# A plan of two pairs a step while the loop fills, and x3 turned at the end of a step

## The reference

```
x = layernorm(x + L1(x, edges))            # for a row: x1 + leaky(scale * p + shift)
x = layernorm(x + L2(x, edges, ...))       # equivariant layer; ssp(x) = softplus(x) - log 2
x = layernorm(x + L3(x, edges))            # q, k, v = x @ W; softmax of q.k over the edges of a source
```

## Time and profile before

| | |
|---|---|
| time, median of 3 runs | 2155.87 us (2149.54 to 2156.42) |
| the profiled execution | 2156.94 us, span 2155.2 us |
| busy share of the span | PE 84%, DVE 67%, ACT 53%, POOL 44% |
| mean granted TensorE clock | 0.896 |
| the last phase | from 1643 us of the span to its end |

### The profile page before, as it was taken

One profiled execution on the slowest core, in us unless ns is written; L12 is line 12 of the kernel. 1 busy time (PEld: TensorE's weight loads), 2 busy tenths in 40 slices (PEclk: granted clock), 3 DMA queues, 4 the chain that ended last, 5 costly groups with the idle time before them and its releaser, 6 DMA issues. The chain is left out here.

```text
span 2155.2 us, 24520 instructions
## 1 busy us (share of the span) xinstructions
PE 1803.9 (84%) x5525; PEld 933.2 (43%) x5525; DVE 1434.7 (67%) x2621; ACT 1149.2 (53%) x2356; POOL 949.1 (44%) x1070
## 2 busy tenths in 40 slices
PE   5999999599999999999999995961881588998840
PEld 2444444244444444444444443531771344544420
DVE  5365554177777777777777773517995578787876
ACT  1344434255555555555555552224883878877853
POOL 2212102166666666656666663544553232333236
PEclk8999999799999999999999997985555689999965
DMA  7752102534444454444444445554556887878774
GB/s 250 250 206 63 27 13 31 142 134 172 171 159 166 157 172 172 165 164 155 169 172 172 163 153 188 105 87 156 110 119 178 257 242 221 238 212 241 200 212 144
DMA packets 167421, 350.61 MB, mean 163 GB/s; under 512 B 30481, under 2 KB 30962, under 8 KB 166838
## 3 DMA queue, kind: packets, MB, share of 16 engines
q1 hardware_dynamic: 130838, 247.28, 32.4%
q0 software_dynamic: 33168, 98.01, 20.4%
q10 hardware_dynamic: 3344, 4.51, 0.7%
HBM read 177.32 MB, written 153.71 MB: 154 GB/s over the span
## 5 line engine op out<-in xcount | busy, mean ns | idle before, releaser
L687 PE MATMUL d_p_h<-w3a,d_xT 128*128 128x512 f32 x632 | 285.6, 595 | 23.2 <-DMA d_xT<-in_xT 23.2
L687 PE MATMUL d_p_p<-d_wr,d_x1T 128*128 128x512 f32 x632 | 288.3, 600 | 0.0
L687 PE MATMUL d_p_o<-d_w,d_uT 128*128 128x512 f32 x632 | 284.5, 593 | 3.0 <-ACT d_uT L762 3.0
L562 POOL TENSOR_SCALAR d_small<-d_mv 128x1 f32<-128x1 f32 x158 | 77.6, 491 | 296.7 <-DVE d_mv L813 148.7
L851 DVE TENSOR_TENSOR d_zz<-d_yg,d_xbeta 128x512 f32<-128x512 f32 x79 | 136.9, 1733 | 96.3 <-POOL d_yg L902 96.3
L687 PEld LDWEIGHTS d_p_h<-w3a,d_xT 128*128 128x128 f32 x632 | 120.7, 191 | 175.6 <-issue 175.6
L687 PEld LDWEIGHTS d_p_o<-d_w,d_uT 128*128 128x128 f32 x632 | 119.8, 190 | 153.7 <-issue 149.1
L755 ACT ACTIVATE d_yn<-d_y,d_small 128x512 f32<-128x512 f32 x79 | 64.3, 814 | 228.2 <-POOL d_small L567 228.2
L687 PEld LDWEIGHTS d_p_p<-d_wr,d_x1T 128*128 128x128 f32 x632 | 115.6, 193 | 116.5 <-issue 116.5
L783 ACT ACTIVATE d_x<-d_zz,d_small 128x512 f32<-128x512 f32 x79 | 64.2, 813 | 174.9 <-POOL d_small L567 174.9
L294 PE MATMUL m_p_H<-m_xT,m_w 128*128 128x512 f32 x320 | 146.8, 613 | 4.8 <-ACT m_xT L335 4.8
(11 more groups left out here) (286 smaller groups left out, 4080.9 us busy)
## 6 DMA issues: line engine op xcount, KB each, us to landing
sum_counted<-m_tile_sum SPq DMA_DIRECT2D x10, 2112.0 KB
state<-d_empty SPq DMA_DIRECT2D x80, 264.0 KB, 2.4
update<-d_empty SPq DMA_DIRECT2D x80, 256.0 KB, 2.3
pair_x<-x SPq DMA_DIRECT2D x40, 512.0 KB
out_rows<-pair_rows SPq DMA_DIRECT2D x40, 512.0 KB
d_xT<-in_xT SPq DMA_DIRECT2D x79, 256.0 KB
d_z<-sum_counted SPq DMA_DIRECT2D x79, 256.0 KB
d_x<-in_x SPq DMA_DIRECT2D x79, 256.0 KB
```

The lines of the kernel that those rows point to most:

```text
L562: nc.gpsimd.tensor_scalar(tmp, var, factor, add, ALU.mult, ALU.add).then_inc(done, 1)
L687: last = nc.tensor.matmul(out[:, :], lhsT[:, c, :], w[:, c, :], start=(c == 0), stop=(c == KB - 1))
```

## The change

PLAIN goes from 3 to 4, so that the first use of all four buffers is a plain load, and the fill of pair 3 and POOL's add for it are gone. `plain_plan` gives 2, 2, 2, 2 and then four times 2, 2, 1, 1, 2, where it gave 3, 3, 2, 2, then 2 and 1 in turn, then 1, 2. `tile_plan` is as it was. On PE and ACT the turns and copies of x3 stand at the end of the step in which x3 was made, and the scalars' turn, copy and second product a step earlier than they did, ahead of PE's `tile_sums` and ACT's late tile.

```diff
@@ -53,7 +53,7 @@
 PLAIN_BUFS = 0
 PAIRS = NODE_TILES // 2
 ROW_BUFS = 4
-PLAIN = 3
+PLAIN = 4
 STATE = ATT + HEADS
 LOG2 = 0.6931471805599453
 BIG = 3.0e38
@@ -1181,7 +1181,7 @@
 
 def plain_plan(steps):
 
-    plan = [3, 3, 2, 2] + [2 - i % 2 for i in range(steps - 6)] + [1, 2]
+    plan = [2] * 4 + [2, 2, 1, 1, 2] * ((steps - 4) // 5)
     assert sum(plan) == PAIRS
     return plan
 
@@ -1217,10 +1217,7 @@
 def pair_fill(nc, k, sp, j):
 
     b = j % ROW_BUFS
-    if j >= ROW_BUFS:
-        sp.wait_ge(k.pair_gone[b], 16 * (j // ROW_BUFS))
-    else:
-        sp.wait_ge(k.quotient_done, 1)
+    sp.wait_ge(k.pair_gone[b], 16 * (j // ROW_BUFS))
     sp.dma_start(k.pair_rows[b][:, :, :], k.quotient[:, :].rearrange("p (a d) -> p a d", a=1).to_broadcast([P, 2, D])
                  ).then_inc(k.pair_filled[b], 16)
 
@@ -1340,7 +1337,6 @@
                 pair_load_p(nc, k, sp, j)
             for j in range(2):
                 pair_load_x1(nc, k, sp, j)
-            pair_fill(nc, k, sp, PLAIN)
             sp.wait_ge(scattered, 16 * T)
 
         @block.gpsimd
@@ -1695,7 +1691,7 @@
                 if step + 2 < T:
                     gather_rows(step + 2)
                 if step + 1 < STEPS:
-                    for j in range(given, given + HERE[step + 1]):
+                    for j in range(max(given, PLAIN), given + HERE[step + 1]):
                         pair_add_p(nc, k, pool, j)
                     given += HERE[step + 1]
             pool.wait_ge(gone, 16 * T)
@@ -1808,25 +1804,25 @@
                 last.then_inc(s_done, 1)
 
             for step in range(STEPS):
-                b, c, d = step - 1, step - 2, step - 3
-                if 0 <= c < T:
-                    turn_x3(c, 0)
-                    turn_x3(c, 1)
-                if 0 <= b < T:
-                    turn_ssp(b)
+                a, b, c, d = step, step - 1, step - 2, step - 3
                 if 0 <= c < T:
                     if c == 0:
                         pe.wait_ge(k.wqk_in, 32)
                     queries(c)
                 if 0 <= d < T:
                     turn_scores(d)
-                if 0 <= b < T:
-                    second(b)
-                if 0 <= d < T:
                     spread_scores(d)
                     values(d)
                 if 0 <= c < T:
                     keys(c)
+
+                if a < T:
+                    turn_ssp(a)
+                if 0 <= b < T:
+                    turn_x3(b, 0)
+                    turn_x3(b, 1)
+                if a < T:
+                    second(a)
                 if 0 <= d < T:
                     tile_sums(d)
 
@@ -1919,21 +1915,14 @@
                 late = HERE[step - 1] if step else 0
                 if 0 <= d < T:
                     away_from(d)
-                if 0 <= c < T:
-                    x3_turned_out(c, 0)
-                    x3_turned_out(c, 1)
                 if 0 <= e < T:
                     state_factors(e)
-                if 0 <= b < T:
-                    ssp_turned_out(b)
                 for u in range(unit, unit + early):
                     tile_normalise(nc, k, act, u)
                 if 0 <= c < T:
                     query_out(c)
                 if 0 <= d < T:
                     scores_out(d)
-                if 0 <= b < T:
-                    second_product_out(b)
                 for u in range(unit + early, unit + early + between):
                     tile_normalise(nc, k, act, u)
                 if a < T:
@@ -1944,6 +1933,13 @@
                     x3_squares(b, 0)
                     x3_squares(b, 1)
                     x3_rows(b)
+                if a < T:
+                    ssp_turned_out(a)
+                if 0 <= b < T:
+                    x3_turned_out(b, 0)
+                    x3_turned_out(b, 1)
+                if a < T:
+                    second_product_out(a)
                 for u in range(unit + early + between, unit + TILES[step]):
                     tile_normalise(nc, k, act, u)
                 unit += TILES[step]
```

## The result

The changed kernel takes 2283.36 us (median of 4 runs, 2282.98 to 2286.03) against 2153.93 before: a ratio of 1.0606 (95% interval 1.0585 to 1.0627), 129 us more. The prediction was 2304 in a range of 2250 to 2350, slower with 0.94. The profiled run took 2286.03, its span is 2284.3.

What follows compares the result with a forecast made beforehand. Waits in a circle set the last phase's pace; after the change the four-buffer ring binds from step 9. Loss 160.5 less 13 gained in the fill, 147.5 on 2156.94, gives 2304.4 us; range 2250 to 2350.

Steps and rivals of the forecast that it cites:

- The count of tiles: Last phase: DVE hands over 3.2 tiles a step, ACT takes 3, four row buffers run out; loss 160.5 us.
- The size of R: Row-buffer ring, last phase: time from a buffer's store through fill and add to DVE's start, taken as 16 us.
- a turn of under 12 us: Row-buffer ring: a turn from store to DVE's start this short was named as showing the forecast wrong.
- R = 13: Row-buffer ring: low case, below every turn seen, as queues are emptier in a stall; chain ends at 400, time 2266 us.
- The chain of the prediction: Last phase: DVE's step starts summed from step 8 as zero to the end of its last pair, 438.7 us.
- The steps without a stall: Last phase from step 8: steps where no pair waits for a buffer last 17.8 us, up from 16.7.
- the sum of 438.7: Step 8 to the end of DVE's last pair: 438.7 us with R = 16, against 278.2 before.
- The fill: Up to the end of step 7: DVE does 14 pairs where it did 16, gaining 13 us (bounds 8.65 and 17.3).
- The turns and copies: End of step on PE and ACT: saves PE's 28.6 us wait, but adds 1 us in each unstalled step.
- The rival of the lower clock: PE drops to its lower clock in stalls, products come late: up to 45 us more, 2349; chance 0.1.
- a ring that comes back faster: Row-buffer ring: store, fill and add take 3.7 us each, R is 11.1, time 2243 us; chance 0.07.
- the rival of the paying turns: Ring does not bind; PE's 28.6 us wait and the fill's 13 come off, 2115 us; chance 0.04.

Runs made afterwards that it cites:

- four runs: Changed kernel with old plan: 2195.22 us; with start of 2 each, then 1.5 pairs a step: 2193.61; with ACT taking up to 4 tiles: 2207.17; with five row buffers: 2192.59.
- the plan alone: Changed kernel with PE's and ACT's loops as before, leaving only the new plan of pairs and the fourth plain pair: 2257.25 us, ratio 1.0461.
- PE kept busy: Kernel before with only the turns and copies moved, plus four unneeded products on PE ahead of the spreading: 2161.77 us, ratio 1.0029.
- the busy PE: Whole changed kernel plus four unneeded products on PE ahead of the spreading: 2276.57 us, ratio 1.0565.
- the turns alone: Kernel before with only the turns and copies of x3 and the scalars' product moved, old plan, three plain pairs: 2194.26 us, ratio 1.016.

## Why the prediction came out as it did

- **The count of tiles**: right, and shown by four runs. The stalls are where it put them: at steps 11, 15, 16, 17, 19 and 20, of 30.1 to 30.9 us where 31 and more were forecast, and 50.4 at 21. DVE's waits for the add were to be over 150 us; they are 145.8 over the phase.
- **The size of R**: mis-sized. I took 16 from turns that were seen in the fill, with 15.0 the shortest. In the stalls up to step 19 it is 12.1 to 14.8, and in steps 20 to 22 11.7 to 11.9; so one of the prediction's own signs of being wrong, a turn of under 12 us, was met. The reason given for R = 13 as a bound, that queues are emptier in a stall, fits what is seen: the DMA is busy 0.64 to 0.78 of the time within the first five of these turns and 0.63 to 0.68 within the last three, against 0.87 and 0.89 within the two of the earlier trace rows. It should have set the value. DVE had waited for both turns of the earlier trace rows, for 4.06 and 0.54 us, so they held no slack at their end; they were longer ahead of the fill (5.31 and 6.71 us behind the store, 2.67 here), and one ahead of the add (7.34 for 3.63). The chain of the prediction ends at 400 with R = 13 and at 388 with R = 12.
- **The steps without a stall**: mis-sized the other way. 17.8 us each was forecast; after has 20.3 at step 9, 18.4 and 18.7 at 12 and 13. The late tile was to end 8.8 behind the weights; in a stall it is 9.4 (2004.39 to 2013.77). These and their like bring the chain to the 411 measured. So the sum of 438.7, too high by 27.6, held two errors of opposite sign: R was worth some -39 to -50 us, the other offsets +11 to +23 (estimates from the chain's two ends). That they partly cancelled was luck.
- **The fill**: 13 us of gain were forecast and 3.9 seen, but the term was right. With the plan alone step 8 begins 12.1 us earlier (1796.70). The turns take 8.2 of that back in the changed kernel, and 16.0 by themselves (1824.80).
- **The turns and copies**: this is the step that failed. "1 us in each step that is not stalled" priced ACT's side of the move only. PE's side was written off with the remark that PE has its queries ready early: what it then does is stand, 1.96 us ahead of the spreading, and fall to its lower clock. They cost 36 us alone, of which 31 come back with PE kept busy, and 26 to 30 in the sum.
- **The rival of the lower clock** (0.1, up to 2349) had the mechanism and the wrong place. It was priced in the stalled steps. There it costs three waits of some 0.25 us, and the busy PE takes 2.3 us off all seven together; it acts with the turns alone, and ahead of step 8, in steps that have no stall, which the rival did not look at.
- **The other rivals**: a ring that comes back faster was priced at R = 11.1 and 2243. R was in fact 11.7 to 14.8, between that rival and the forecast. That the time came out 18 us from the forecast and 40 from the rival is luck in part: the turns cost more than was thought and made up for the shorter ring. PE's 28.6 us of wait did go, as the rival of the paying turns had it, and were worth nothing.

What stays open: how the turns' 18 us behind step 8 that a busy PE does not return come about, what limits steps of 17.4 and 18.9 us once PE's clock is kept up, and how the 16 us that the turns cost in steps 0 to 7 divide between clock and place (with four products 10 of them come back with the turns alone, and 6.5 of 8.2 in the changed kernel). That PE be kept busy ahead of the scalars' turn in a stalled step was not tried.

## What to carry to other kernels

Count what each engine hands over and what the next one takes, step by step, over the whole loop: a surplus of 0.2 tiles a step shows nowhere in a busy share, and costs nothing until it has filled the ring; then each further pair pays the full turn of the ring. Take the time of that turn at the load that it will meet: the same chain of transfers took at least 15.0 us in the full loop here and 11.7 to 14.8 in the stalls. And when work is moved so that an engine no longer waits in one place, ask where it will wait instead: for TensorE, a wait of 2 us a step in a new place cost some 31 us here through the clock, and removing the old wait of 28.6 us gained nothing.

## What the runs showed of the hardware

TensorE stood 1.96 us in each step of 20.4, and ran the eight products behind that pause partly or wholly at the lower of its levels (5.16 to 6.75 us in the steps read, for 3.70); that so short a pause should go with it I had not expected. Products that nobody needs, 1.8 or 3.6 us of them a step in the same place, kept the clock at 0.96 to 1.00 and brought 31 us of 36 back. The three transfers of the ring took 11.7 to 11.9 us together with the DMA engines busy 0.63 to 0.68 of that time, 12.1 to 14.8 at 0.64 to 0.78, and 15.0 and 19.7 at 0.89 and 0.87. The load was not varied by itself, and a part of the longer turns is the order on POOL.
